# Slots past the first 32 of an expert layer: a chain on VectorE spread over several slots with its products on GpSimd, and sixteen owner comparisons made one

## The reference

```
logits = xf @ gate_w.T                    # 1024 tokens x 32 experts
w, idx = top_k(logits, 2); w = softmax(w)
out = sum over experts e of  combine[:, e] * (xf @ W[e].T + b[e])
x = x + tanh(g_ffn[1]) * out
```

## Time and profile before

| what | value |
|---|---|
| runs | 917.05 us (median of 3; 916.7 to 919.35) |
| span of the profiled execution | 912.7 us |
| own time of the profiled execution | given on the page only as its span |
| PE busy | 840.6 us (92%) |
| DVE busy | 656.2 us (72%) |
| ACT busy | 397.0 us (43%) |
| POOL busy | 427.1 us (47%) |

### The profile page before, as it was taken

The page is one execution under the profiler, slowest core; times in us unless marked ns, Lnnn a source line. Parts: engine busy times, 40 slices in busy tenths (PEclk is TensorE's granted clock), DMA queues, the critical chain, the costliest instruction groups (busy, mean ns, idle before and its releaser), DMA issues. The chain is left out here.

```text
span 912.7 us, 13118 instructions
## 1 busy us (share of the span) xinstructions
PE 840.6 (92%) x4337; PEld 702.5 (77%) x4337; DVE 656.2 (72%) x1300; ACT 397.0 (43%) x1009; POOL 427.1 (47%) x386
## 2 busy tenths in 40 slices
PE   5878999999999999999999999977989999989990
PEld 4766888888888888888888888866878687777870
DVE  3776888766778876778876688774473557999975
ACT  4634334333424424325333433434124446878970
POOL 5488447535436634635733643512020048876730
PEclk9999999999999999999999999998999969999995
DMA  8302101101101100200300120006100556999817
GB/s 333 155 1 93 70 1 59 59 1 47 70 1 46 69 0 0 77 39 0 115 0 0 46 92 1 1 1 239 55 1 12 205 211 223 356 333 342 324 38 277
DMA packets 23641, 91.13 MB, mean 100 GB/s; under 512 B 6576, under 2 KB 7088, under 8 KB 15776
## 3 DMA queue, kind: packets, MB, share of 16 engines
q1 hardware_dynamic: 17440, 81.00, 24.1%
q0 software_dynamic: 6144, 9.46, 2.9%
HBM read 86.23 MB, written 14.68 MB: 111 GB/s over the span
## 5 line engine op out<-in xcount | busy, mean ns | idle before, releaser
L361 POOL TENSOR_TENSOR qT<-straight,turned 128x512 f32<-128x512 f32 x64 | 82.5, 1290 | 147.5 <-DVE turned L572 147.5
L458 ACT ACTIVATE probs<-bank,negmax 128x128 f32<-128x128 f32 x256 | 90.5, 365 | 130.3 <-DVE negmax L583 130.2
L572 DVE TENSOR_TENSOR turned<-bank,sinT 64x512 f32<-64x512 f32 x160 | 110.2, 688 | 2.2
L134 PE MATMUL bank<-wo_hi,oT_hi 128*128 128x512 f32 x256 | 101.3, 396 | 8.0 <-DVE oT_lo L596 6.2
L134 PE MATMUL bank<-xT_hi,wq_hi 128*128 128x512 f32 x256 | 105.7, 413 | 1.1 <-POOL wq_lo L340 1.1
L135 PE MATMUL bank<-xT_lo,wq_hi 128*128 128x512 f32 x256 | 101.5, 397 | 0.0
L136 PE MATMUL bank<-xT_hi,wq_lo 128*128 128x512 f32 x256 | 101.3, 396 | 0.0
L135 PE MATMUL bank<-wo_lo,oT_hi 128*128 128x512 f32 x256 | 100.6, 393 | 0.0
L136 PE MATMUL bank<-wo_hi,oT_lo 128*128 128x512 f32 x256 | 100.6, 393 | 0.0
L465 ACT ACTIVATE pT_hi<-bank 128x512 fp32r<-128x512 f32 x64 | 38.3, 598 | 133.1 <-PE bank L738 133.1
L570 DVE TENSOR_TENSOR straight<-bank,cosT 128x512 f32<-128x512 f32 x80 | 55.3, 691 | 48.2 <-PE bank L136 43.7
(11 more groups left out here) (228 smaller groups left out, 2101.3 us busy)
## 6 DMA issues: line engine op xcount, KB each, us to landing
ring<-in_ew SPq DMA_DIRECT2D x28, 1024.0 KB, 8.5
raw_big<-in_wq SPq DMA_DIRECT2D x8, 1024.0 KB, 4.8
raw_big<-in_wo SPq DMA_DIRECT2D x8, 1024.0 KB, 4.8
early_w<-in_ew SPq DMA_DIRECT2D x8, 1024.0 KB, 8.1
ring<-picked SPq DMA_DIRECT2D x8, 512.0 KB, 7.3
raw_k<-in_wk SPq DMA_DIRECT2D x8, 256.0 KB, 5.0
ctx_raw<-in_ctxT SPq DMA_DIRECT2D x4, 512.0 KB, 5.9
raw_v<-in_wv SPq DMA_DIRECT2D x8, 256.0 KB, 4.8
```

The costliest lines, as they stand in the source:

```text
L134: nc.tensor.matmul(out_, hi, r_hi, start=start, stop=False)
L361: nc.gpsimd.tensor_tensor(dst, straight[:, k, :], turned[:, k, :], ALU.add).then_inc(rope_sum, 1)
L458: ex = nc.scalar.activation(probs[:, u % 2, h, :], bank_scores[u % 2][:, h * S:(h + 1) * S], ACT.Exp, bias=negmax[:, u % UNITS, h:h + 1], ...
L572: last = nc.vector.tensor_tensor(turned[dst, k, :], bank[src, :], sinT[src, tok], ALU.mult)
```

## The change

`far_slots` is cut into pieces that are numbered by the semaphore far_built. The two products, the addition, the comparison with zero (now an operation of its own, over_full) and the product with it go to GpSimd: the first behind give 1, three behind give 4, the last behind give 8. The sum of far_weighted stays on VectorE, after slot 5, and the comparison in_far after slot 9. TensorE waits for all seven steps. `owners` becomes one comparison of 16 x 32 elements with broadcast operands after slot 16, the sum after slot 17, and the two conversions after slot 18; owners_ready counts to four.

```diff
--- before.py
+++ after.py
@@ -895,6 +895,7 @@
         rank_i, full_i, rest_i = (sb(n, [P, NB * TOP], I32) for n in ("rank_i", "full_i", "rest_i"))
         full, rest, far_slot = (sb(n, [P, NB * TOP]) for n in ("full", "rest", "far_slot"))
         owner = sb("owner", [P, 16])
+        over_full = sb("over_full", [P, 16])
 
         f_turned, f_hi, f_lo, f_mm, f_sum, f_added = (sem(f"f_{n}") for n in ("turned", "hi", "lo", "mm", "sum", "added"))
         g_bias, g_ctx, g_gate = (sem(f"g_in_{n}") for n in ("bias", "ctx", "gate"))
@@ -915,6 +916,9 @@
         y_in = [sem(f"y_in{t}") for t in TILES]
         y_added2 = sem("y_added2")
         REST = range(ALWAYS, SLOTS)
+        summed_to = upto[:, 1, 16:]
+        FAR_PIECES = {1: (0,), 4: (2, 3, 4), 8: (6,)}
+        FAR_BUILT, OWNED = 7, 4
 
 
         def item(i):
@@ -1007,7 +1011,7 @@
 
                 for k in range(RING, NX):
                     weights(k, k)
-                sp.wait_ge(owners_ready, 1)
+                sp.wait_ge(owners_ready, OWNED)
                 for k in range(NX, ALWAYS):
                     extra_weights(k)
                 given(ALWAYS)
@@ -1079,6 +1083,27 @@
                     pool.wait_ge(e_kept, k + 1)
                     pool.indirect_dma_start(out=picked, out_offset=bass.IndirectOffsetOnAxis(ap=place_row[:, k:k + 1].bitcast(U32), axis=0),
                                             in_=result[:, lane, :], in_offset=None, bounds_check=TOP * T - 1, oob_is_err=False).then_inc(y_out[lane], 16)
+
+                def far_slots(n):
+
+                    pairs = [P, NB * TOP, NX]
+                    shown = [P, NB * TOP, 16]
+                    pool.wait_ge(far_counted, 2)
+                    if n:
+                        pool.wait_ge(far_built, n)
+                    if n == 0:
+                        op = nc.gpsimd.tensor_tensor(far_weighted[:, :, :], onehot[:, :, :, :].bitcast(F32).rearrange("p t k e -> p (t k) e"),
+                                                     first_far[:, :].unsqueeze(1).broadcast_to(pairs), ALU.mult)
+                    elif n == 2:
+                        op = nc.gpsimd.tensor_tensor(far_slot[:, :], far_slot[:, :], full[:, :], ALU.add)
+                    elif n == 3:
+                        op = nc.gpsimd.tensor_scalar(over_full[:, :], full[:, :], 0.0, None, ALU.is_gt)
+                    elif n == 4:
+                        op = nc.gpsimd.tensor_tensor(far_slot[:, :], far_slot[:, :], over_full[:, :], ALU.mult)
+                    else:
+                        op = nc.gpsimd.tensor_tensor(far_code[:, :, :], in_far[:, :, :],
+                                                     pair_codes[:, :, :].rearrange("p t k -> p (t k)").unsqueeze(2).broadcast_to(shown), ALU.mult)
+                    op.then_inc(far_built, 1)
 
                 pool.wait_ge(f_added, NB)
                 nc.gpsimd.memset(ones_raw[:, :], 1.0).then_inc(constants, 1)
@@ -1104,7 +1129,9 @@
                     if k + TAKEN < ALWAYS:
                         take(k + TAKEN)
                     give(k)
-                pool.wait_ge(owners_ready, 1)
+                    for n in FAR_PIECES.get(k, ()):
+                        far_slots(n)
+                pool.wait_ge(owners_ready, OWNED)
                 with if_needed(pool):
                     for k in REST[:TAKEN]:
                         take(k)
@@ -1259,7 +1286,7 @@
                     if COMB <= k < COMB + NB:
                         comb_kept(k - COMB)
                     one(k, ALWAYS)
-                act.wait_ge(owners_ready, 1)
+                act.wait_ge(owners_ready, OWNED)
                 with if_needed(act):
                     expert_upper(ALWAYS, 0)
                     expert_upper(ALWAYS, 1)
@@ -1394,8 +1421,6 @@
                     dve.wait_ge(rows_ready, n + 1)
                     nc.vector.tensor_scalar(place_token[:, cols], place_row[:, cols], NOWHERE | (T - 1), None, ALU.bitwise_and).then_inc(tokens_ready, 1)
 
-                summed_to = upto[:, 1, 16:]
-
                 def far_starts():
 
                     step(nc.vector.memset(upto[:, :, 0:16], 0.0))
@@ -1416,42 +1441,24 @@
                         src, dst, by = n % 2, (n + 1) % 2, 1 << n
                         step(nc.vector.tensor_tensor(upto[:, dst, 16:], upto[:, src, 16:], upto[:, src, 16 - by:16 + NX - by], ALU.add))
                         ready()
-                    step(nc.vector.tensor_tensor(first_far[:, :], summed_to, last_full_i[:, :], ALU.subtract))
-
-                def far_slots():
-
-                    pairs = [P, NB * TOP, NX]
-                    ready()
-                    step(nc.vector.tensor_tensor(far_weighted[:, :, :], onehot[:, :, :, :].bitcast(F32).rearrange("p t k e -> p (t k) e"),
-                                                 first_far[:, :].unsqueeze(1).broadcast_to(pairs), ALU.mult))
-                    ready()
-                    step(nc.vector.tensor_reduce(far_slot[:, :], far_weighted[:, :, :], AX.X, ALU.add))
-                    ready()
-                    step(nc.vector.tensor_tensor(far_slot[:, :], far_slot[:, :], full[:, :], ALU.add))
-                    ready()
-                    step(nc.vector.scalar_tensor_tensor(far_slot[:, :], full[:, :], 0.0, far_slot[:, :], ALU.is_gt, ALU.mult))
-                    ready()
-                    step(nc.vector.tensor_tensor(in_far[:, :, :], numbers[:, 1:17].unsqueeze(1).broadcast_to([P, NB * TOP, 16]),
-                                                 far_slot[:, :].unsqueeze(2).broadcast_to([P, NB * TOP, 16]), ALU.is_equal))
-                    ready()
-                    nc.vector.tensor_tensor(far_code[:, :, :], in_far[:, :, :],
-                                            pair_codes[:, :, :].rearrange("p t k -> p (t k)").unsqueeze(2).broadcast_to([P, NB * TOP, 16]),
-                                            ALU.mult).then_inc(far_built, 1)
+                    nc.vector.tensor_tensor(first_far[:, :], summed_to, last_full_i[:, :], ALU.subtract).then_inc(far_counted, 1)
 
                 def far_places(half):
                     pairs = slice(half * NB, half * NB + NB)
                     nc.vector.tensor_tensor(at_far[:, pairs, :], numbers[:, :].unsqueeze(1).broadcast_to([P, NB, P]),
                                             rest[:, pairs].unsqueeze(2).broadcast_to([P, NB, P]), ALU.is_equal).then_inc(far_at, 1)
 
-                def owners():
-                    for j in range(16):
-                        last = nc.vector.tensor_scalar(passed[:, j, :], summed_to, float(j), None, ALU.is_le)
-                    step(last)
-                    ready()
-                    step(nc.vector.tensor_reduce(owner[:, :], passed[:, :, :], AX.X, ALU.add))
-                    ready()
-                    nc.vector.tensor_copy(owner_at[:, 16:17], summed_to[:, NX - 1:NX])
-                    nc.vector.tensor_scalar(owner_at[:, 0:16], owner[:, :], float(NX - 1), None, ALU.min).then_inc(owners_ready, 1)
+                def owners(n):
+                    if n:
+                        dve.wait_ge(owners_ready, n)
+                    if n == 0:
+                        nc.vector.tensor_tensor(passed[:, :, :], summed_to.unsqueeze(1).broadcast_to([P, 16, NX]),
+                                                numbers[:, 0:16].unsqueeze(2).broadcast_to([P, 16, NX]), ALU.is_le).then_inc(owners_ready, 1)
+                    elif n == 1:
+                        nc.vector.tensor_reduce(owner[:, :], passed[:, :, :], AX.X, ALU.add).then_inc(owners_ready, 1)
+                    else:
+                        nc.vector.tensor_copy(owner_at[:, 16:17], summed_to[:, NX - 1:NX]).then_inc(owners_ready, 1)
+                        nc.vector.tensor_scalar(owner_at[:, 0:16], owner[:, :], float(NX - 1), None, ALU.min).then_inc(owners_ready, 1)
 
                 def turned_rest(k):
                     dve.wait_ge(t_hi, k + 1)
@@ -1507,16 +1514,21 @@
                     one(k, ALWAYS)
                     if COMB <= k < COMB + NB:
                         add_bias(k - COMB)
-                    if k == 10:
-                        far_slots()
+                    if k == 5:
+                        dve.wait_ge(far_built, 1)
+                        nc.vector.tensor_reduce(far_slot[:, :], far_weighted[:, :, :], AX.X, ALU.add).then_inc(far_built, 1)
+                    if k == 9:
+                        dve.wait_ge(far_built, 5)
+                        nc.vector.tensor_tensor(in_far[:, :, :], numbers[:, 1:17].unsqueeze(1).broadcast_to([P, NB * TOP, 16]),
+                                                far_slot[:, :].unsqueeze(2).broadcast_to([P, NB * TOP, 16]), ALU.is_equal).then_inc(far_built, 1)
+                    if k in (16, 17, 18):
+                        owners(k - 16)
                     if k in (11, 12):
                         far_places(k - 11)
                     if k == 15:
                         dve.wait_ge(far_laid, 1)
```

(8 more changed lines are left out.)

## The result

The changed kernel is slower: 920.5 us against 917.3 (medians of 22 runs each, 915.23 to 924.0 and 913.23 to 923.63). The ratio is 1.0032 with a 95% interval of 1.0019 to 1.0046, some 2.9 us. Forecast was 915.5 us, with a range up to 919.0.

What follows compares the result with a forecast made beforehand. TensorE was taken to pace the expert stage at 3.265 us a slot, with late landings of gives as second limit. Slots up to 14 at 0.0 and owners at minus 1.55 gave 915.5 us from 917.05; range 913.4 to 919.0.

Steps and rivals of the forecast that it cites:

- the owners' minus 1.55 us: Slots 16 to 18: with the owners' work spread, TensorE loses 0.45 us instead of 2.01, minus 1.55 us.
- the chain's part, put at 0.0: Slots up to 14: the chain's 2.06 us at slot 12 is paid beforehand by waits for landings, so 0.0.
- the first stated bound: Owners' part, slots 16 to 18: nothing lost by TensorE, minus 2.0 us.
- Late next is again VectorE's remainder, then TensorE itself: Behind slot 14: landings of gives 9 and 10 no longer late, so VectorE and then TensorE set the pace.
- I take 0.6 of the delay: Gives 2 and on: landings move by 0.6 of the later issue, 1.3, 1.75 and 2.3 us.
- the second rival: Slots 9 to 14: the whole delay of the gives lands, plus 1.3 us by slot 14, 916.8 us; chance 0.18.
- the first rival: Gives on the DMA engines: their queue hides GpSimd's delay, landings stay, minus 1.6 us, 913.9 us in all; chance 0.22.
- The three operations on 16 elements: GpSimd behind give 4: 0.21 us each and some 0.06 for each semaphore, 0.8 us.
- The 512-element product: GpSimd behind give 1: 2.0 us beside VectorE's subtractions plus 0.15 to get going, 2.15 us.
- The last product: GpSimd behind give 8: the 256-element product, 0.73 to 1.1 us beside VectorE, 0.9 taken.
- The third rival: GpSimd becomes the pace: its backlog does not drain by slot 14, 3.0 us more to slot 27, 919.8 us; chance 0.08.
- The 4.35 us: Around the profiled span: difference between the 912.7 us span and the 917.05 us median, carried to the forecast.

Runs made afterwards that it cites:

- chain_only: The changed kernel with the old owners code in one piece after slot 16, so the chain's part alone; 1.0022 of the kernel before (1.0003 to 1.0041).
- owners_only: The kernel before with the owners part alone, the chain left in one piece after slot 10; 1.0003 of the kernel before (0.9983 to 1.0022).
- product_load: The kernel before plus only a 512-element product on GpSimd behind give 1, into a buffer nobody reads; 1.0001 of the kernel before (0.9982 to 1.002).
- early_both: The kernel before with the chain in one VectorE piece ahead of slot 0's turned rows and owners over three slots, four lanes; 0.9991 of the kernel before.
- gpsimd_load: The kernel before plus five GpSimd operations of the change's shapes and places, into a buffer nobody reads; 1.0032 of the kernel before (1.0012 to 1.0052).
- memset_load: The kernel before plus GpSimd fills, which read no operand, behind gives 1, 4 and 8; 1.0050 of the kernel before (1.0027 to 1.0073).
- early_lanes6: early_both with six lanes of results instead of four; 0.9960 of the kernel before (0.9945 to 0.9974), 912.9 us.

## Why the prediction was wrong

Two steps of its sum failed: the owners' minus 1.55 us did not reach the end of the kernel, and the chain's part, put at 0.0, cost some 2.0 us (chain_only, 0.3 to 3.8).

- **The owners' part, minus 1.55 us.** The shorter stage came as forecast: slots 14 to 18 became 2.0 us shorter, the first stated bound, and slots 18 to 25 0.2 us longer. What failed is the step from a shorter stage to a shorter kernel. "Late next is again VectorE's remainder, then TensorE itself" left out the landings behind slot 18. Those of gives 21 to 24 took 9.0 to 9.8 us before and 10.4 to 12.1 after, and slots 25 to 31 gave 1.5 us back (owners_only 1.0003; with six lanes 0.9966 against 0.9981). The chain's part lengthens these slots too (21.41 us in chain_only), and how the two divide is open.
- **"I take 0.6 of the delay", slots up to 14: 0.0.** The share was not the same for all gives. Counted from the start of slot 2, give 6 was issued 4.4 to 5.3 us later than in the two profiles of before and landed 4.6 to 4.7 us later, so about the whole delay landed there, as the second rival had it, and that rival was given 0.18. Give 5, issued 4.8 to 5.9 us later, landed only 1.9 to 3.6 later. The row that 0.6 was taken from, give 14, was one in which VectorE and so the weights' loads had paused too; a pause of GpSimd alone is another case. The rule on taking turns between queues, cited with the first rival, is not decided by any run; what it would have favoured did not happen.
- **The three operations on 16 elements, taken at 0.8 us.** Mis-sized: give 5 came 2.5 to 2.7 us later behind give 4 than before. Their price in the rows was that of an operation beside additions of 32 elements on VectorE; here two of the three ran beside a subtraction of 1024 and lasted 0.87 and 1.15 us, 0.7 and 0.95 longer. The 512-element product was priced too high: 2.15 us taken, 1.31 long, and give 2 came 1.6 us later behind give 1. The last product, taken at 0.9, lasted 1.47 us and put 0.9 to 1.0 between gives 8 and 9.
- **No cost on VectorE from GpSimd.** The prediction bounded how much longer GpSimd takes beside VectorE, and never asked the opposite. Its row had gone one way: the product of 2.01 us at 754.90 stood beside the subtraction of the row below, which lasted 1.21. Here the subtraction went from 1.22 to 2.80 us, and slots 2 to 5 took 1.38 us more. The Trainium skill, GPSIMD Engine Reference, "Specifications", says that GpSimd shares its SBUF interfaces with VectorE and contends with its instructions of two SBUF inputs; the trace agrees (2.80 us beside the product, 1.26 at most in the kernel with fills). product_load finds no loss of time from this alone, within 1.8 us.

```profile
754.79 1.21 DVE L1464 TENSOR_TENSOR cT_lo<-early_w,cT_hi 128x1024 fp32r<-128x1024 f32 x1
```

- **The sum.** The second rival's mechanism is what the changed kernel's profile shows in slots 5 to 14, with 5 us of delay instead of 3.85, and the give-back of slots 25 to 31 came on top. The third rival, a backlog that never drains, did not occur: GpSimd idles again for 0.94 us before give 14. The 4.35 us do not all lie around the span either: in the changed kernel's profiled execution it is 1.8 (920.01 us against 918.2), so the execution shown before was a quick one. To carry the difference to the median was still right.
- **Right:** that the chain's 2.06 us would not be won, even with the idle time ahead of slot 12 gone (chain_only has none there, and its slots 5 to 14 are no shorter), and that landings are what takes them (early_both, with nothing of the chain on either engine once slot 0 has begun, does not win them either); ScalarE's waits for landings, forecast at about 9 us, 8.2 found; that no new wait between the engines costs (gpsimd_load has none of them and loses the same).

What stays open is how the loss of 2.9 us divides. gpsimd_load and the change agree, but the interval of gpsimd_load alone is 3.7 us wide, and slots 5 to 14 differ by up to 2.4 us between executions of the same code. ScalarE's waits for landings do not follow the times closely either: 5.3 us in gpsimd_load, which loses 2.9 us, and 13.3 in early_both, which loses nothing. Why memset_load loses more than gpsimd_load (1.0050 against 1.0032, intervals overlapping) is not settled.

## What to carry to other kernels

An engine that is half idle can still be late: look at how long after the result that it waits for each of its DMAs is issued, and where results wait for a landing, before giving it arithmetic. Where a buffer's lanes wait for landings on nearly full DMA engines, a stall removed upstream comes back downstream; widen the lanes first, then remove the stalls (early_both 0.9991, early_lanes6 0.9960). Price an operation on GpSimd from both sides, its own length and that of VectorE's operation beside it. And before reading a stage off one profile, see how far profiles of unchanged code differ there.

## What the runs showed that was not expected

- A 512-element product on GpSimd of 1.30 to 1.31 us makes the VectorE subtraction beside it 2.73 to 2.80 us long in all seven kernels that have it; fills of 0.95 us lengthen none.
- On the other side, an addition of 16 elements on GpSimd that starts within a VectorE subtraction takes 0.87 or 0.88 us, in the five profiles that have it, against 0.2 for a product of eight elements. It ends 0.07 us after the subtraction each time. The product of 16 elements behind it does the same where it starts within a subtraction (1.15 us), and takes 0.21 and 0.23 us in the two profiles in which VectorE is not subtracting then.
- The time from issue to landing of the same 128-row DMA lies between 2.3 and 18.0 us: 2.3 to 2.6 near 872 us of the kernel before, where the DMA share is 0.10 to 0.15, and 18.0 near 845 us of early_lanes6, where it is 1.0. With half the weights' traffic it is 6.3 at most in the gives of the stage.
